# A decoder layer with routed experts: first expert for the last token tile without scatter and read, down bias stacked and added in memory, weight remainders and last rank in another order

## The chip, the cores and the metric

The kernel runs on one core of a Trainium2 chip. Its metric is the device time of one execution in microseconds (us). The engines are TensorE (PE, with its weight loads as PEld), VectorE (DVE), ScalarE (ACT), GpSimd (POOL) and SyncE (SP, which issues most DMAs). Each works through its own list in order and waits on semaphores.

## The reference

One layer of three parts, each added to its input and normalised: causal self-attention with 16 heads, a cross-attention with a linear feature map, and a mixture of 8 experts of which each token takes 2. There are 8 x 112 = 896 tokens of 512 numbers. The part that the change touches is the last:

```python
logits = h @ router_weight.T + router_bias
top_vals, top_idx = jax.lax.top_k(logits, TOP_K)
top_w = jax.nn.softmax(top_vals, axis=-1)
scores = jnp.zeros_like(logits).at[jnp.arange(T)[:, None], top_idx].set(top_w)
...
glu = gate * jax.nn.sigmoid(gate * ALPHA)
act = (up + 1.0) * glu
expert_out = jnp.einsum('eti,eih->eth', act, down_proj) + down_proj_bias[:, None, :]
out = jnp.einsum('te,eth->th', scores, expert_out)
```

## The kernel before, in words

The 896 tokens are 7 tiles of 128 (NT = 7); a row of 512 numbers is KC = 4 blocks of 128. Weights and operands of the large products are split into a high part (rounded to fp32r, by ACT: `split_hi`) and a remainder (by DVE: `split_lo`, line 1420); `products` (line 315) runs three matmuls per block, high x high, high x remainder, remainder x high. So weights of an expert are ready when ACT (`gu_high`, `dn_high`) and DVE (`gu_low`, `dn_low`) have been over them.

Routing goes tile by tile: `cross_out` and `cross_add` finish the second part, `x2_norm(n)` writes the tile's row, PE turns it (`turn_x2`, line 799), ACT copies it (`x2_copy`), PE computes the logits (`router`, line 806), DVE picks two experts (`choose`, lines 1623 to 1647), PE ranks the tokens (`rank`, lines 816 and 817), DVE computes slots and scores (`assign`, lines 1653 to 1668), and POOL scatters each row twice into `x_rows` in memory (`scatter`, line 508). Each expert has a region of ROWS slots there; the first CAP = 288 are read for it. After the scatter of all seven tiles SP reads experts 0 to 2 (`rows_in`, lines 431 and 433), then the scores and token numbers (`meta`, line 440). The order of these steps on PSUM banks is written out in `route_order`.

The down bias is handled ahead of the experts: scores are transposed (`turn_scores`, `scores_high`, `scores_low`), `down_bias(n)` multiplies them by the 8 x 512 bias in three matmuls over 8 partitions, DVE adds the row (`bias_add`, line 1673), and SP stores the sum as the start of `y_acc` in memory (`base_store`).

Then the experts. For expert e, PE transposes the rows read (`gather(e, k)`, line 973, three pieces of 128, 128 and 32 rows; ACT and DVE make high part and remainder), runs four parts of 24 matmuls (`gate_up_part(e, q)`), and the down products of the expert before (`down(e - 1, k)`, 36 matmuls). For each part DVE clamps (`clamp`, lines 1900 and 1904), ACT takes the sigmoid, POOL multiplies (`gated`, line 529), DVE multiplies again (`hidden`, line 1913), and ACT and DVE split the result (`h_high`, `h_low`). ACT scales the down results (`y_evac`, line 1329) and POOL adds them to `y_acc` with an indirect DMA (`add_rows`, line 546). Banks 0 to 3 hold the parts, 4 to 7 gathers and down results. Expert 7 is combined by one-hot matmuls with rows of `y_acc` read back, and the last normalisation and the stores follow.

On ACT and DVE the order inside an expert is written out by hand; `SPLITS` says behind which part the next expert's gate and up weights are split. On DVE it ends with the last `gu_low`s and `dn_low(e)`, on ACT with the `gu_high`s, `y_evac(e-1, 0)`, `y_evac(e-1, 1)`, `dn_high(e)`, `y_evac(e-1, 2)`.

## Time and profile before

| what | value |
|---|---|
| median of three timed runs | 865.51 us (865.08 to 868.34) |
| the profiled execution | 868.03 us, span 866.2 us |
| busy PE, PEld | 836.4 us (97%), 734.4 us (85%) |
| busy DVE, ACT, POOL | 479.2 us (55%), 319.2 us (37%), 97.2 us (11%) |
| mean granted TensorE clock | 0.98 |
| DMA | 97.39 MB, mean 112 GB/s |

The span runs from the first to the last instruction of the profiled execution; a little lies around it. A busy PE is not PE at its peak: matmuls are pipelined, and a matmul at half the clock counts as busy for twice as long. The page draws the span in 40 slices with the granted clock of each. The chain that ended last gives 11% of the span to PE at line 315 and 1% each to DVE's split of weights at line 1420 and to the reads of the down weights. Waits are given as idle time ahead of an instruction with the one that ended it.

### The profile page before, as it was taken

How to read it: one execution, taken by the hardware profiler on the slowest of the kernel's cores; microseconds unless marked ns; L12 is line 12 of the kernel's file. 1: busy time of each engine (PE TensorE's matmuls, PEld its weight loads, DVE VectorE, ACT ScalarE, POOL GpSimd, SP SyncE). 2: the span in 40 equal slices, each digit the busy share in tenths (PEclk: the TensorE clock that was granted, in tenths of full speed). 3: DMA queues.
4: the chain of work that ended last, by engine and by line, in shares of the span. 5: the costliest groups of instructions: out<-in, count | busy, mean ns of one | idle time of the engine just before them, and what ended most of it. 6: DMA issues, size and time to landing. Idle time of an engine off the chain costs nothing. (4 is left out here: it accounts for less than half of the span.)

```text
span 866.2 us, 12601 instructions
## 1 busy us (share of the span) xinstructions
PE 836.4 (97%) x4913; PEld 734.4 (85%) x4913; DVE 479.2 (55%) x877; ACT 319.2 (37%) x718; POOL 97.2 (11%) x92
## 2 busy tenths in 40 slices
PE   7999999999999999999999999999988999999995
PEld 6989898989899898978799878888866888888883
DVE  4435445363635464484860343455677677777765
ACT  4443324242333333342352222122233365555434
POOL 0000000000000000000000000110221244343331
PEclk9999999999999999999999999999975999999998
DMA  9990644614030003003110011110187366665225
GB/s 322 345 298 6 200 136 140 192 55 148 6 98 6 25 8 122 1 6 133 50 36 0 2 36 36 61 48 14 61 330 223 125 201 195 178 198 160 65 49 184
DMA packets 35758, 97.39 MB, mean 112 GB/s; under 512 B 6664, under 2 KB 9224, under 8 KB 33008
## 3 DMA queue, kind: packets, MB, share of 16 engines
q1 hardware_dynamic: 32224, 88.69, 30.5%
q0 software_dynamic: 3472, 7.87, 4.5%
q8 instruction: 40, 0.66, 0.3%
q14 instruction: 22, 0.18, 0.1%
HBM read 64.10 MB, written 31.53 MB: 110 GB/s over the span
## 5 line engine op out<-in xcount | busy, mean ns | idle before, releaser
L315 PE MATMUL bank<-w_kv,cT 128*125 128x512 f32 x576 | 143.5, 400 | 0.0
L315 PE MATMUL bank<-xT,w_qkv 128*128 128x512 f32 (+1 forms) x672 | 137.8, 365 | 0.2 <-ACT qT L1117 0.2
L315 PEld LDWEIGHTS bank<-xT,w_qkv 128*128 128x128 f32 x672 | 122.1, 188 | 15.2 <-ACT qT L1117 0.5
L315 PEld LDWEIGHTS bank<-w_kv,cT 128*125 128x125 f32 x576 | 104.1, 186 | 23.7
L315 PE MATMUL bank<-x_g,w_gu 128*128 128x288 f32 x768 | 109.7, 301 | 3.6 <-DVE x_g L1420 2.9
L315 PEld LDWEIGHTS bank<-x_g,w_gu 128*128 128x128 f32 x768 | 105.5, 192 | 5.5 <-issue 3.2
L499 POOL TENSOR_TENSOR ln_rs<-ln_ve,half 128x1 f32<-128x1 f32 (+2 forms) x16 | 11.2, 704 | 628.6 <-DVE ln_ve L1549 614.9
L315 PE MATMUL bank<-w_o,zT 128*128 128x512 f32 x336 | 79.8, 395 | 0.5 <-DVE acc L1755 0.5
L315 PE MATMUL bank<-w_qkv,xT 128*128 128x256 f32 x588 | 77.3, 287 | 0.0
L315 PEld LDWEIGHTS bank<-w_o,zT 128*128 128x128 f32 x336 | 61.7, 188 | 15.1 <-DVE acc L1454 1.8
L315 PEld LDWEIGHTS bank<-w_qkv,xT 128*128 128x128 f32 x588 | 72.2, 191 | 0.0
L315 PE MATMUL bank<-w_dn,hT 128*128 128x512 f32 (+1 forms) x288 | 68.5, 396 | 0.0
L315 PEld LDWEIGHTS bank<-w_dn,hT 128*128 128x128 f32 (+1 forms) x288 | 46.0, 161 | 19.3
L1420 DVE TENSOR_TENSOR w_qkv<-raw_w,w_qkv 128x1024 fp32r<-128x1024 f32 x21 | 25.7, 1225 | 60.5 <-ACT w_qkv L1085 60.5
L1127 ACT ACTIVATE prob<-prob,neg_max 112x112 f32<-112x112 f32 x128 | 47.8, 375 | 21.9 <-DVE neg_max L1471 21.9
L1154 ACT ACTIVATE relu_c<-bank 125x512 f32<-125x512 f32 x24 | 14.4, 598 | 111.0 <-PE bank L315 111.0
L1137 ACT CAST zT<-bank 128x448 fp32r<-128x448 f32 x32 | 17.0, 533 | 92.5 <-PE bank L695 92.5
L1420 DVE TENSOR_TENSOR w_gu<-raw_gu,w_gu 128x1024 fp32r<-128x1024 f32 x32 | 48.4, 1523 | 0.5 <-ACT w_gu L1085 0.5
L1454 DVE TENSOR_TENSOR acc<-acc,bank 128x512 f32<-128x512 f32 x49 | 33.6, 685 | 24.3 <-PE bank L315 24.3
L1515 DVE SCALAR_TENSOR_TENSOR phi_k<-exp_c,relu_c 125x512 f32<-125x512 f32 x24 | 16.6, 691 | 48.1 <-ACT exp_c L1155 48.1
L529 POOL TENSOR_TENSOR pr<-gl,sg 128x288 f32<-128x288 f32 x32 | 32.8, 1025 | 87.7 <-ACT sg L1318 87.5
L1443 DVE COPY V<-bank 128x512 f32<-128x512 f32 (+1 forms) x32 | 20.0, 625 | 39.9 <-PE bank L315 39.9
(171 smaller groups left out, 1206.8 us busy)
## 6 DMA issues: line engine op xcount, KB each, us to landing
x_rows<-blank SPq DMA_DIRECT2D x9, 2084.0 KB, 15.6
raw_gu<-in_w_gu_dram SPq DMA_DIRECT2D x8, 2048.0 KB, 7.8
raw_w<-in_w_qkv_dram SPq DMA_DIRECT2D x22, 512.0 KB, 8.3
raw_dn<-in_w_down_dram SPq DMA_DIRECT2D x8, 1024.0 KB, 9.4
raw_c<-in_ctx_t_dram SPq DMA_DIRECT2D x8, 750.0 KB, 4.4
raw_o<-in_w_o_dram SPq DMA_DIRECT2D x8, 512.0 KB, 4.1
xg<-x_rows SPq DMA_DIRECT2D x8, 512.0 KB, 5.7
raw_kv<-in_w_kv_dram SPq DMA_DIRECT2D x2, 1024.0 KB, 6.8
```

The costliest lines, as they stand in the source:

```text
L315: last = nc.tensor.matmul(mm_out, lhs(a, k), rhs(b, k), start=(k == 0 and i == 0), stop=(k == n - 1 and i == 2))
L499: nc.gpsimd.tensor_tensor(ln_rs[:, ln, n0:n1], ln_ve[:, ln, n0:n1], half[:, n0:n1], ALU.pow)\
L529: nc.gpsimd.tensor_tensor(pr[:, q % 2], gl[:, q % 2], sg[:, q % 2], ALU.mult)\
L1127: e = nc.scalar.activation(prob[0:S, g, j, :], prob[0:S, g, j, :], ACT.Exp, bias=neg_max[0:S, i:i + 1], scale=-1.0, accum_out=exp_sum[0:S, ...
L1137: nc.scalar.copy(zT[:, 0, h, hf * HALF:(hf + 1) * HALF], banks[6 + g % 2][:, 0:HALF])\
L1154: nc.scalar.activation(relu_c[0:CM, n % 2, :], bank("ck", n)[0:CM, :], ACT.Relu)
L1420: return nc.vector.tensor_tensor(dst, src, bits(hi), ALU.subtract)
L1443: nc.vector.tensor_copy(V[:, p % 2, 2 * j:2 * j + n, :], banks[(1 + j) % 2][:, 0:n * 2 * E].rearrange("p (a c) -> p a c", a=n))\
L1454: nc.vector.tensor_tensor(acc[:, n, :], acc[:, n, :], banks[n % 2][:, :], ALU.add)\
L1515: nc.vector.scalar_tensor_tensor(phi_k[0:CM, n % 3, :], exp_c[0:CM, n % 2, :], 1.0, relu_c[0:CM, n % 2, :], ALU.min, ALU.add).then_inc(m[" ...
```

## The change

Expert 0 of the last tile (END = 6) leaves the common way. Its 128 tokens go through expert 0 as a dense tile straight from the turned row `x2T`: `x_end` (high part by ACT, remainder by DVE), 24 products of 128x512 and two bias matmuls from a one-row bias `bias_end` into banks 1 and 3 (`end_gate_up`), clamp, sigmoid and products (`end_clamp`, `end_swish`, `end_hidden`), a turn into bank 6 (`end_turn`), split (`end_h_high`, `end_h_low`), 12 down products into bank 0 (`end_down`) and a scaled add into the tile's bias row (`end_add`). For these tokens the slot of expert 0 is one past all regions (`offs_end`), and they are not counted there. Expert 0's rows can thus be read after six tiles' scatters (`row_out`); experts 1 and 2 wait for the seventh (`end_out`).

The down bias becomes one matmul over 72 partitions: the scores stand three times (`score3`), the bias as high part, remainder and high part. ACT copies the result (`bias_copy`), the base stored to `y_acc` is the row alone, and POOL adds the bias to it by an indirect add (`add_bias`). `add_rows` waits for seven adds more (ADDED).

The order changes: `choose(5)` stands before `x2_norm(6)`, `rank(6)` inside the dense products, the split of weights of expert 0 and 1 elsewhere, expert 1's gathers one part later, a sigmoid early on ACT. Cut to its core:

```diff
-            last = [("rk", 4), ("st", 0), ("t1", 5), ("rt", 5), ("t1", 6), ("rk", 5), ("rt", 6), ("db", 0), ("rk", 6),
-                    ("cnt", 0), ("db", 1), ("db", 2), ("st", 1), ("db", 3), ("db", 4), ("db", 5), ("db", 6)]
+            last = [("rk", 4), ("st", 0), ("t1", 5), ("rt", 5), ("db", 0), ("rk", 5), ("t1", 6), ("rt", 6), ("rk", 6),
+                    ("db", 1), ("st", 1), ("db", 2), ("db", 3), ("db", 4), ("db", 5), ("db", 6), ("cnt", 0)]
-        SPLITS = {0: ((3,), (), (), (), ()), 1: ((), (), (), (0,), (1, 2, 3))}
+        SPLITS = {0: ((1,), (2,), (3,), (), ()), 1: ((), (), (), (0,), (1, 2, 3))}
@@ SP
             def base_store(n):
-                sp.wait_ge(*done("db", n))
-                sp.dma_start(y_acc[n * P:(n + 1) * P, :], acc[:, n, :]).then_inc(base_out, 16)
+                sp.wait_ge(m["row_ok"], n + 1)
+                sp.dma_start(y_acc[n * P:(n + 1) * P, :], row[:, n, 0:D]).then_inc(base_out, 16)
...
+                sp.dma_start(bias_end[0:1, :].rearrange("o (c p) -> o c p", p=P),
+                             t["gu_b"].rearrange("p e c -> e c p")[0:1]).then_inc(in_bias, 16)
...
-            sp.wait_ge(*ready("wo", NT - 1))
-            sp.dma_start(raw_gu[1], t["w_gu"][1]).then_inc(in_gu[1], 16)
...
-            sp.wait_ge(row_out, 16 * 2 * NT)
-            for e in range(3):
+            for n in range(4, NT):
+                base_store(n)
+            sp.wait_ge(row_out, 16 * 2 * END)
+            rows_in(xg[0], 0, in_xg[0])
+            sp.wait_ge(*ready("wo", NT - 1))
+            sp.dma_start(raw_gu[1], t["w_gu"][1]).then_inc(in_gu[1], 16)
+            sp.wait_ge(end_out, 16 * 2)
+            for e in range(1, 3):
@@ POOL
+            def add_bias(n):
+                if n < END:
+                    pool.wait_ge(*done("db", n))
+                else:
+                    pool.wait_ge(m["end_dve"], 7)
+                nc.gpsimd.indirect_dma_start(y_acc, bass.IndirectOffsetOnAxis(ap=ids[:, n:n + 1], axis=0),
+                                             acc[:, n, :], None, bounds_check=T + DUMP - 1, oob_is_err=True,
+                                             compute_op=ALU.add).then_inc(add_done, 16)
+            pool.wait_ge(base_out, 16 * (NT + 1))
+            for n in range(4):
+                add_bias(n)
             for e in range(NE + 1):
                 if e < NE:
                     for q in range(KC):
                         gated(e, q)
+                        if e == 0 and 4 + q < END:
+                            add_bias(4 + q)
                 if e == 1:
-                    pool.wait_ge(base_out, 16 * (NT + 1))
+                    add_bias(END)
                     pool.wait_ge(in_meta, 64)
                 if e and e < NE:
                     add_rows(e - 1, lambda k, rows: meta[0:rows, k, e - 1, NE:NE + 1], lambda k: (3 * (e - 1) + k) % 4)
@@ PE, down bias and the dense tile
-                products(o[:, :], lambda a, k: scoreT[a][0:NE, n * P:(n + 1) * P], lambda b, k: dn_b[b][0:NE, :], 1)\
+                nc.tensor.matmul(o[:, :], scoreT[0:STACK, n * P:(n + 1) * P], dn_b[0:STACK, :], start=True, stop=True)\
...
+            end_gate_up(0, 0, 0, 2)
             rank(6)
+            end_gate_up(0, 0, 2, KC)
             down_bias(1)
+            pe.wait_ge(m["end_dve"], 1)
+            pe.wait_ge(in_bias, 16)
+            end_gate_up(1, 0)
+            for h in range(2):
+                nc.tensor.matmul(banks[END_BANK[h]][:, :], all_ones[0:1, :], bias_end[0:1, h * D:(h + 1) * D],
+                                 start=False, stop=False)
+            turn_scores(1)
             down_bias(2)
+            down_bias(3)
@@ PE, experts
+            gather(0, 0)
+            gather(0, 1)
+            pe.wait_ge(m["gu_lo"], KC)
+            end_gate_up(0, 1).then_inc(m["end_mm"], 1)
+            down_bias(4)
+            down_bias(5)
+            gather(0, 2)
+            down_bias(6)
+            count()
             for e in range(NE):
                 pe.wait_ge(m["gu_lo"], KC * e + KC)
                 pe.wait_ge(m["xg_lo"], 3 * e + 3)
                 for q in range(KC):
+                    if e == 0 and q == 1:
+                        pe.wait_ge(m["end_dve"], 3)
+                    if e == 2 and q == 0:
+                        pe.wait_ge(m["end_dve"], 7)
                     gate_up_part(e, w_gu[e % 2], x_g[e % 2], q)
-                    if e == 0 and q + 1 < KC:
-                        gather(1, q)
-                    if q and e and e + 1 < NE:
+                    if e == 0 and q == 0:
+                        end_turn()
+                    if q and e + 1 < NE:
                         gather(e + 1, q - 1)
+                if e == 1:
+                    end_down()
                 if e:
                     for k in range(3):
                         down(e - 1, k)
@@ ACT, before and at the start of the experts
             x2_copy(5)
+            gu_high(0, 0, 2)
+            gu_high(0, 0, 3)
+            top_tanh(5)
             x2_copy(6)
...
+            split_hi(x_end[:, 0], x2T[:, END % 2]).then_inc(m["end_act"], 1)
+            bias_copy(0)
...
+            bias_copy(4)
+            bias_copy(5)
+            gather_high(0, 2)
+            end_swish()
+            bias_copy(6)
+            gu_high(1, 1, 0)
+            end_h_high()
@@ DVE
             cross_stats(6)
+            choose(5)
             x2_norm(6)
-            choose(5)
             assign(5)
+            gu_low(0, 0, 0)
+            split_lo(x_end[:, 1], x2T[:, END % 2], x_end[:, 0]).then_inc(m["end_dve"], 1)
             choose(6)
+            gu_low(0, 0, 1)
             assign(6)
...
+            gather_low(0, 0)
+            gather_low(0, 1)
+            gather_low(0, 2)
+            end_clamp()
+            levels()
+            end_hidden()
+            gu_low(1, 1, 0)
...
                 if more:
                     dn_low(e, e % 2)
+                if e == 1:
+                    end_add()
```

## Rows read from the trace of the kernel before

**Rows 1.** The page: the span, and PE's line of part 1.
```profile
span 866.2 us, 12601 instructions
...
PE 836.4 (97%) x4913; PEld 734.4 (85%) x4913; DVE 479.2 (55%) x877; ACT 319.2 (37%) x718; POOL 97.2 (11%) x92
```

**Rows 2.** The chain in order of time: start, us, what (count).
```profile
719.23 14.93 PE bank L315 x84
...
741.97 14.93 PE bank L315 x84
```

**Rows 3.** Timeline of the last tiles: start, us, engine, line, operation [idle before <-releaser].
```profile
639.97 0.55 DVE L1554 TENSOR_SCALAR row<-acc,ln_mv,ln_rs 128x512 f32<-128x512 f32 x1 [0.69 <-POOL ln_rs L499]
...
643.44 0.17 DVE L1668 CAST slot_u<-slot_f 128x2 uint32<-128x2 f32 x1
...
644.50 0.17 DVE L1623 TENSOR_TENSOR logit<-bank,rt_b 128x8 f32<-128x8 f32 x1 [0.90 <-PE bank L806]
...
647.66 0.17 DVE L1668 CAST slot_u<-slot_f 128x2 uint32<-128x2 f32 x1
...
648.63 0.97 POOL L508 DMA_INDIRECT x_rows<-row,slot_u  x1 [1.88 <-DVE slot_u L1668]
...
653.72 0.38 SPq L431 DMA_DIRECT2D xg<-x_rows  x1
...
658.97 2.50 PE L973 MATMUL bank<-ident,xg 128*128 128x128 f32 x12 [2.55 <-DMA xg<-x_rows]
```

**Rows 4.** Busy time by stretch: stretch, us, PE, PEld, DVE, ACT, POOL, clock, DMA.
```profile
640.00:641.00 1.00, 0.42 (x2) 0.43 (x3) 0.93 (x6) 0.00 (x0) 0.00 (x0) 0.54 1.03 442
667.00:668.00 1.00, 1.00 (x8) 1.00 (x7) 0.05 (x1) 0.00 (x0) 0.00 (x0) 0.81 1.04 371
855.00:857.00 2.00, 1.16 (x6) 0.62 (x4) 1.93 (x8) 1.73 (x4) 1.04 (x2) 1.00 0.28 101
858.00:859.00 1.00, 0.00 (x0) 0.00 (x0) 0.96 (x7) 1.00 (x3) 0.54 (x1) 0.76 0.17 62
```

**Rows 5.** Timeline of PE in expert 0.
```profile
662.60 5.56 PE L315 MATMUL bank<-x_g,w_gu 128*128 128x288 f32 x24 [1.13 <-DVE x_g L1420]
...
668.36 3.44 PE L315 MATMUL bank<-x_g,w_gu 128*128 128x288 f32 x24
...
680.94 6.64 PE L315 MATMUL bank<-x_g,w_gu 128*128 128x288 f32 x48 [1.77 <-DVE x_g L1420]
```

**Rows 6.** Indirect DMAs by stretch (725, 704 to 705, 646): count, us to landing.
```profile
y_acc<-y,meta POOLq DMA_INDIRECT x1, 4.9
...
y_acc<-y,meta POOLq DMA_INDIRECT x1, 7.8
...
x_rows<-row,slot_u POOLq DMA_INDIRECT x1, 2.9
```

**Rows 7.** Groups by line and shape: PE at line 729, count, busy us, mean ns.
```profile
L729 PE MATMUL bank<-v_c,phi_k 125*128 125x132 f32 x192 | 25.7, 278 | 0.0
```

**Rows 8.** Timeline from expert 1 to expert 2.
```profile
695.61 8.61 PE L315 MATMUL bank<-w_dn,hT 128*128 128x512 f32 x36
...
704.12 1.89 ACT L1085 CAST w_dn<-raw_dn 128x2048 fp32r<-128x2048 f32 x1
...
704.75 6.67 PE L315 MATMUL bank<-x_g,w_gu 128*128 128x288 f32 x48 [0.53 <-DVE w_gu L1420]
...
706.04 2.29 DVE L1420 TENSOR_TENSOR w_dn<-raw_dn,w_dn 128x2048 fp32r<-128x2048 f32 x1 [1.35 <-ACT w_dn L1085]
```

**Rows 9.** Timeline of POOL, DVE and PE in experts 2 and 3.
```profile
711.12 2.42 POOL L529 TENSOR_TENSOR pr<-gl,sg 128x288 f32<-128x288 f32 x2
...
712.41 0.46 DVE L1913 SCALAR_TENSOR_TENSOR hh<-up,pr 128x288 f32<-128x288 f32 x1
...
718.80 0.43 PE L973 MATMUL bank<-ident,xg 32*128 32x32 f32 x4
...
727.18 1.54 POOL L546 DMA_INDIRECT y_acc<-y,meta  x1 [0.30 <-issue]
```

More of the change, by code:

```diff
@@ L240, in decoder_layer @@
         row_out = sem("row_out")
+        end_out = sem("end_out")
         add_done = sem("add_done")
@@ L1192, in top_tanh, with bias_copy @@
                     .then_inc(m["tw_ok"], 1)
+            def bias_copy(n):
+                act.wait_ge(*ready("db", n))
+                act.wait_ge(m["row_ok"], n + 1)
+                nc.scalar.copy(acc[:, n, :], bank("db", n)[:, :]).then_inc(done("db", n)[0], 1)
             def scores_high(i):
@@ L1359, in _ @@
                         dn_high(e, e % 2)
-                if e and more:
+                if more:
                     gather_high(e + 1, 2)
@@ L1873, in _, with levels @@
-            bias_add(1)
-            gu_low(0, 0, 0)
-            scores_low(1)
-            bias_add(2)
-            gu_low(0, 0, 1)
-            bias_add(3)
-            gu_low(0, 0, 2)
-            bias_add(4)
-            gu_low(0, 0, 3)
+            gu_low(0, 0, 2)
+            gu_low(0, 0, 3)
+            scores_low(1)
+            def levels():
+                dve.wait_ge(*ready("cnt", 0))
+                nc.vector.tensor_reduce(most[:, 0:1], bank("cnt", 0)[:, 0:NE], AX.X, ALU.max)\
+                    .then_inc(done("cnt", 0)[0], 1)
+                dve.wait_ge(*done("cnt", 0))
+                for j in range(ROUNDS - 1):
+                    nc.vector.tensor_scalar(most[:, j + 1:j + 2], most[:, 0:1], float((j + 1) * CAP), None, ALU.is_gt)\
+                        .then_inc(m["put_ok"], 1)
+                dve.wait_ge(m["put_ok"], 3 * NT + ROUNDS - 1)
+                nc.vector.tensor_reduce(most[:, 4:5], most[:, 1:4], AX.X, ALU.add).then_inc(m["put_ok"], 1)
+                dve.wait_ge(m["put_ok"], 3 * NT + ROUNDS)
+                nc.vector.tensor_copy(more_i[:, :], most[:, 4:5]).then_inc(m["more_ok"], 1)
@@ new lines, in end_h_low, with end_add @@
+            def end_h_low():
+                dve.wait_ge(m["end_act"], 3)
+                split_lo(h_end[:, 1], banks[6][:, :].rearrange("p (k c) -> p k c", k=KC), h_end[:, 0])\
+                    .then_inc(m["end_dve"], 1)
+            def end_add():
+                dve.wait_ge(m["end_mm"], 3)
+                dve.wait_ge(*done("db", END))
+                nc.vector.scalar_tensor_tensor(acc[:, END, :], banks[0][:, :], row[:, END, D:D + 1], acc[:, END, :],
+                                               ALU.mult, ALU.add).then_inc(m["end_dve"], 1)
@@ L1942, in _ @@
                 hidden(e, KC - 1)
-                if e and more:
+                if more:
                     gather_low(e + 1, 2)
```

204 lines of the change are left out of this document (123 added, 81 removed).

## The prediction, made before the changed kernel was built

> **What bounds the kernel now.** I read the page first, then the chain that ended last, then the stretch 636 to 720 us engine by engine. The span is 866.2 us [rows 1]; the profiled execution took 868.03 us, the three timed ones 865.08 to 868.34, median 865.51. Below I work out a difference in us and add it to span and median alike.
>
> TensorE (PE) is busy 97% of the span [rows 1], and from expert 2 on the chain of waits repeats with PE products from one expert to the next, 719.23 and 741.97, so 22.74 us an expert [rows 2]. No gap of PE there is large enough to repay a delay, so whatever time PE loses or wins before expert 3 should reach the end unchanged. That leaves one place where the change works: from the last token tile's router to expert 3.
>
> There the reader is to see three things. First, PE waits for the scatter: the last tile's slots are ready at 647.83, its first scatter starts at 648.63, the read of expert 0's rows is issued at 653.72, and PE gets them at 658.97 [rows 3]. Second, the granted clock falls to 1.2 GHz at 640.5, after a stretch of little matrix work, and is back at 2.4 GHz only at 667.2 [rows 4], 4.6 us after the dense products began at 662.60 [rows 5]. Third, expert 0 to expert 1 costs PE another 1.77 us of waiting for the remainder of expert 1's rows [rows 5].
>
> **Start of expert 0 (S0).** The change reads expert 0's rows after six tiles. The sixth tile's slots are ready at about 643.6 [rows 3], so with two issues and a landing of 2.9 us [rows 6] the read goes out near 649, and with the 5.2 us between read and first transpose [rows 3] the rows are there at 654. The wait for DMA is gone. What is late next is PE and ACT work, which I walk through. VectorE (DVE) now does choose(5) (ten small instructions of 0.1 to 0.2 us, an estimate of 1.2) before x2_norm(6), so the last row is ready at 641.7, not 640.5. From row to logits it was 4.0 us [rows 3], with one rank more in front 4.2: the logits come at 645.9. PE then puts 8 of the new 128x512 products around rank(6). 24 matmuls of 288 columns take 5.56 us nearly all at the low clock, 3.44 at the high one [rows 5]; 36 of 512 columns take 8.61 at the high one [rows 8]. So 512 columns cost 0.24 us high and 0.41 low. Eight products, rank and one bias matmul are 3.3 + 1.0 + 0.4 = 4.7 us, to 650.6. With the 4.6 us seen before, the clock comes back just then. The rest at 0.24: 8 products 1.9; two bias matmuls in plain f32, which come as two instructions each, 192 of 132 columns taking 25.7 us [rows 7], hence 0.14 each and about 0.45 at 512 columns, 1.8 together; transposed scores 0.4, two bias products 0.5, two gathers 0.7, 8 products 1.9, two bias products 0.4: 658.2. ACT then copies two bias tiles (0.6 each) before the third gather's copy, and DVE takes its remainder: 660.0, S0 = 660.2, 2.4 us early. If the short matmuls of rank(6) delay the clock by one more step it is 661.2. I take 2.0 early. Bounds: with the high clock throughout, DVE and ACT alone put S0 at 657.4 (5.2 early); with the low clock throughout it is 665 (2.5 late).
>
> **What the removal of bias work is worth.** 21 matmuls become 7; at the low clock 14 x 0.41 = 5.7 us of PE. But they stood in front of rows that only arrived at 658.97, so before, they cost nothing, and now they make room for the 26 added products. The seven adds of DVE become seven copies on ACT (0.6 each, in the walk above) and seven indirect adds on POOL. Splits of weights that move from before 657 into expert 0 (gu_high and gu_low of expert 1) lie beside 3.3 us parts and hide there. The row-wise bias of the last tile is read in 4-byte pieces and is one DMA with many packets; it has from 626 to 652 and delays only weights needed after 680. The three down-bias loads, memsets, wider score copies and earlier base stores (rows, not sums) are free by the same cover. If none of that holds, it is at most 1 us at S0.
>
> **Expert 0 to expert 1 (S1).** From 668.36 to 679.17 PE ran three parts and two of the gathers between them [rows 5], 3.6 us a part with gather, so four parts and three gathers take 14.2 us. New is the turn of the last tile's hidden rows behind part 0: DVE has clamp, levels and hidden products of about 3.6 us to do first, so PE waits 0.4 and turns for 0.4. Expert 1's gathers all move one part later, the last behind part 3, and there no down product covers them: two clamps, two hidden products, two remainders of rows and one of hidden rows at 0.3 to 0.7 each on DVE leave PE idle an estimated 3.4 us. 14.2 + 0.8 + 3.4 = 18.4 us. Before, S0 to S1 was 662.60 to 680.94, 18.34 [rows 5]. What the clock gives is eaten by the uncovered gathers: S1 stays 2.0 early, at 678.9.
>
> **Expert 1 to expert 2 (S2): +5.0.** Before, from S1: down products at +14.67, 36 of them in 8.61 us, expert 2 at +23.81 after 0.53 of waiting [rows 8]. Now 12 products of the last tile go first, a third of 8.61, 2.87 us. Expert 2 also waits for end_add, because the last tile's sum lies in bank 0. end_add stands on DVE behind dn_low(1), which waits for dn_high(1) on ACT, which stands behind y_evac(0,1), which waits for the second down piece. From S1: 14.67 + 3 x 2.87 = 23.28; copy 0.7; dn_high 1.89; dn_low 2.29 [rows 8]; end_add 0.7 (as other 128x512 adds): 28.85. That is 5.04 us more than 23.81. Nothing pays it back, as expert 2 has no idle PE time.
>
> **POOL in expert 2: +4.7.** add_bias(6) waits for end_add too, and add_rows(0) behind it waits for the landing of all seven bias adds. Behind these on POOL's queue stand three adds and then gated(2,0), for which DVE's hidden(2,0) waits. From S2: end_add -0.1, start 0.8 later (slots 647.83 to scatter 648.63 [rows 3]), landing L, wake 0.3, three adds at 1.54 + 0.30 [rows 9], gate an estimated 0.9: 7.4 + L. Before, hidden(2,0) ran at 712.41, 7.66 after S2 at 704.75, just after the first of the two gates that began at 711.12 [rows 9]. From there DVE had no slack: hidden, remainder of weights, clamp, remainder of rows, and PE's gather(3,2) starts at 718.80 in the instant the last of them ends [rows 9]. So PE stalls L - 0.2. Indirect adds landed 4.9 us after issue with quiet queues, 7.8 beside a weight load, scatters 2.9 [rows 6]. I take 4.9, as the nearest in kind: +4.7, bounds +2.7 and +7.6.
>
> The Trainium skill, DMA: Bandwidth & Descriptors, section "Anatomy of one DMA", gives about 2.0 us plus size over 436 GB/s for one such DMA, an estimate of 2.6 us for these 256 KB. The trace's 4.9 speaks against it; by the page the term would be +2.4 and the whole 873.2 (rival 1 takes it in).
>
> **The clock again: +2.3.** After PE's last matmul at about 856.2 the clock fell at 858.8 [rows 4]. The 4.7 us stall is longer than that stretch; if the clock falls in it, the low level would last as after 662.60, 4.6 us at half speed, 2.3 us. The waits of 3.4 and 2.7 us may or may not fall so; I count none. Bounds of this term 0 and 4.6.
>
> **Sum.** -2.0 + 5.0 + 4.7 + 2.3 = +10.0 us: span 876.2, median 875.5.
>
> **Rivals.**
> 1. The landing is hidden or short. For it: scatters landed in 2.9. Against: the adds took 4.9 and more [rows 6]. POOL's term and the fall of the clock go away or shrink: -2.0 + 5.0 = +3.0, 868.5; with half of it, 871.
> 2. It is faster. One mechanism: the added dense products hold or regain the high clock before 648. Then S0 is 5.2 early, expert 0's first part is already fast and its tail hides; the start is worth up to 5.2 + 2.1 + 1.77 = 9.1 us (first part 5.56 against 3.44, and the idle of 1.77 [rows 5]), against +5.0: -4.1, 861.4; with ACT and DVE also done 2.4 us earlier at S2, since their splits there start earlier, 859, which I take for it. It decides only if the clock is up before 648 and POOL's landing is covered. Against: it falls at 640.5, before any new product.
> 3. More of the same: the clock also falls in the waits before S1 and S2, or the add lands beside the 1 MB weight load in 7.8 us. 10.0 + 2.3 + 2.9 = +15.2, 880.7.
> 4. The change does not do what it says: the early read queues behind base stores, or the clock stays low through 660, and S0 is not early at all but up to 2.5 late. 10.0 + 2 to 4.5: 877.5 to 880.
>
> **How the numbers follow.** Forecast 0.52; rival 1 0.22; rival 2 0.06; rival 3 0.12; rival 4 0.08. The range holds the forecast, rival 1, rival 4 and the near half of rival 3: 867.5 to 881. A measurement of this kernel tells some 0.5% (4.3 us) from no change: 861.2 to 869.8 is "same". Faster gets rival 2 and a rest, 0.06; same gets the part of rival 1 without any stall and some of the forecast's low edge, 0.2; slower 0.74.
>
> **What would show it.** In the profile after: PE's first part of expert 0 near 660.6 at the high clock; the granted clock back at 650 to 654; 18.4 us from there to expert 1; 28.9 us from expert 1 to expert 2 with PE's wait put down to DVE's add into the last tile's row; POOL idle before three adds in expert 2 on a DMA's landing; PE idle 4 to 5 us before the small gather of expert 3; then 22.8 us per expert. The prediction is wrong if end_add ends before the down pieces do, if POOL's gates of expert 2 run before DVE wants them, or if the clock never falls to begin with.

## The result, and the profile after

| | before | after |
|---|---|---|
| median of the runs | 865.36 us (865.08 to 868.34, 4 runs) | 880.72 us (880.49 to 881.28, 4 runs) |
| ratio to before | | 1.017, 95% interval 1.0157 to 1.0183 |
| the profiled execution, its span | 868.03 us, 866.2 | 881.28 us, 879.5 |

The change costs 15.4 us where 10 were forecast. The page of the kernel after, the lines that answer to [rows 1]:

```profile
span 879.5 us, 12708 instructions
...
PE 843.1 (96%) x4943; PEld 740.0 (84%) x4943; DVE 482.1 (55%) x889; ACT 324.9 (37%) x729; POOL 106.3 (12%) x99
```

TensorE (PE) has only 6.7 us more of busy time than in [rows 1], on a span 13.3 us longer. About half of the loss is new idle time, and some of the rest is products that ran at half the clock. To find the places, I read the start of the same step in both traces. S0 to S3 are the starts of experts 0 to 3 on PE.

| point on PE | before | after | later by | this step alone | forecast for the step |
|---|---|---|---|---|---|
| S0 | 662.60 | 662.51 | -0.1 | -0.1 | -2.0 |
| S1 | 680.94 | 681.97 | +1.0 | +1.1 | 0 |
| S2 | 704.75 | 712.94 | +8.2 | +7.2 | +5.0 |
| small gather of expert 3 | 718.80 | 731.60 | +12.8 | +4.6 | +4.7 |
| S3 | 727.60 | 741.90 | +14.3 | +1.5 | +2.3 |

From S3 on the delay goes through to the end, but for 1 us that the tail of the profiled execution gives back. The medians are 15.4 us apart and not 13.3, because the profiled execution of before lay 2.7 us above its median and that of after 0.6.

**The start.** Timeline of PE in the kernel after, the last tile up to S0 (start, us, engine, line, operation [idle before <-releaser]), against [rows 3, 5]:

```profile
643.20 1.88 PE L843 MATMUL bank<-rt_w,x2T 128*128 128x8 f32 x8 [0.67 <-ACT x2T L1271]
...
649.77 3.62 PE L1004 MATMUL bank<-w_gu,x_end 128*128 128x512 f32 x8
653.31 1.98 PE L1021 MATMUL bank<-bias_end,all_ones 1*128 1x512 f32 x4
...
656.06 1.32 PE L1044 MATMUL bank<-ident,xg 128*128 128x128 f32 x8
657.03 3.50 PE L1004 MATMUL bank<-w_gu,x_end 128*128 128x512 f32 x8
...
662.51 0.76 PE L326 MATMUL bank<-x_g,w_gu 128*128 128x288 f32 x4 [0.60 <-DVE x_g L1528]
```

The wait for DMA of [rows 3] (2.55 us before the first transposes) is gone, as intended: the transposes at 656.06 wait for nothing. But eight products of 512 columns took 3.50 us at 657.03. Busy time by stretch of the same kernel (the clock is the third figure from the end) tells why, beside [rows 4]:

```profile
642.00:643.00 1.00, 0.53 (x4) 0.29 (x4) 0.97 (x8) 0.44 (x1) 0.00 (x0) 1.00 1.02 394
643.00:644.00 1.00, 0.80 (x4) 0.80 (x4) 1.00 (x2) 0.97 (x3) 0.52 (x1) 0.51 1.00 382
652.00:653.00 1.00, 1.00 (x4) 0.56 (x2) 0.00 (x0) 0.00 (x0) 0.79 (x1) 0.50 0.99 363
653.00:654.00 1.00, 1.00 (x3) 0.44 (x3) 0.00 (x0) 0.00 (x0) 0.78 (x1) 0.87 1.00 369
656.00:657.00 1.00, 1.00 (x9) 0.94 (x8) 0.56 (x1) 1.00 (x3) 0.00 (x0) 0.84 1.14 325
659.00:660.00 1.00, 1.00 (x4) 0.81 (x3) 0.03 (x1) 0.00 (x0) 0.69 (x2) 0.50 0.98 254
660.00:661.00 1.00, 1.00 (x5) 0.52 (x5) 0.00 (x0) 0.20 (x1) 0.90 (x1) 0.96 1.13 213
...
680.00:681.00 1.00, 0.00 (x0) 0.00 (x0) 0.76 (x2) 0.37 (x2) 0.00 (x0) 0.78 0.88 377
...
731.00:732.00 1.00, 0.40 (x4) 0.40 (x4) 1.00 (x3) 0.10 (x1) 0.00 (x0) 0.88 0.95 410
```

The granted clock falls to 1.2 GHz at 643.0 and is back at 2.4 GHz at about 653.2. It is low once more from 656.7 to 660.0, and this time PE had been busy without a gap. The last two rows belong to later stages: the clock falls at about 680.6, in the wait before expert 1, and at about 731.8.

**The loads.** Issues of GpSimd (POOL) and SyncE's queue (SPq) in the kernel after:

```profile
648.01 0.38 SPq L450 DMA_DIRECT2D xg<-x_rows  x1
...
649.38 1.25 POOL L531 DMA_INDIRECT x_rows<-row,slot_u  x1 [3.31 <-DVE score L1782]
649.47 0.42 SPq L459 DMA_DIRECT2D raw_gu<-in_w_gu_dram  x1
650.93 0.97 POOL L531 DMA_INDIRECT x_rows<-row,slot_u  x1 [0.30 <-ACT acc L1282]
...
660.79 0.38 SPq L450 DMA_DIRECT2D xg<-x_rows  x1
```

The last tile is scattered by two indirect DMAs, at 649.38 and 650.93. The landing of the first (from issue, us), against the 2.9 of [rows 6]:

```profile
x_rows<-row,slot_u POOLq DMA_INDIRECT x1, 9.9
```

Expert 0's rows are read at 648.0, one us sooner than I forecast. But the 2 MB load of expert 1's weights now goes out at 649.47, in the same instant as the last tile's scatter. The scatter lands 9.9 us after issue, its second half 9.8, at 660.7, and expert 1's rows, whose read waits for both, are asked for at 660.79. I had not looked at this at all.

**Expert 0 to expert 2.** Timeline of PE, ScalarE (ACT) and VectorE (DVE), kernel after, against [rows 5, 8]:

```profile
677.73 0.43 PE L1044 MATMUL bank<-ident,xg 32*128 32x32 f32 x4 [0.85 <-DVE x_g L1528]
681.97 9.05 PE L326 MATMUL bank<-x_g,w_gu 128*128 128x288 f32 x48 [3.81 <-issue]
...
698.57 3.04 PE L326 MATMUL bank<-w_dn,h_end 128*128 128x512 f32 x12
701.45 8.50 PE L326 MATMUL bank<-w_dn,hT 128*128 128x512 f32 x36
...
707.80 1.89 ACT L1170 CAST w_dn<-raw_dn 128x2048 fp32r<-128x2048 f32 x1
709.73 2.29 DVE L1528 TENSOR_TENSOR w_dn<-raw_dn,w_dn 128x2048 fp32r<-128x2048 f32 x1 [2.06 <-ACT w_dn L1170]
711.94 0.74 DVE L2019 SCALAR_TENSOR_TENSOR acc<-bank,row,acc 128x512 f32<-128x512 f32 x1
712.94 6.62 PE L326 MATMUL bank<-x_g,w_gu 128*128 128x288 f32 x48 [3.00 <-DVE acc L2019]
```

The reader is to see two things: the last four rows are the chain high part of the down weights (ACT), remainder (DVE), `end_add` (DVE), expert 2 (PE), link by link; and two parts of expert 1 took 9.05 us where those of expert 2 took 6.62, because the clock fell in the 3.81 us of waiting.

**POOL in expert 2.** The rows that answer to [rows 9]:

```profile
713.46 1.56 POOL L578 DMA_INDIRECT y_acc<-acc,ids  x1 [13.16 <-DVE acc L2019]
...
719.47 1.58 POOL L568 DMA_INDIRECT y_acc<-y,meta  x1 [4.45 <-issue]
...
724.12 2.04 POOL L552 TENSOR_TENSOR pr<-gl,sg 128x288 f32<-128x288 f32 x2
725.43 1.05 DVE L2052 SCALAR_TENSOR_TENSOR hh<-up,pr 128x288 f32<-128x288 f32 x1 [4.89 <-POOL pr L552]
...
731.60 0.54 PE L1044 MATMUL bank<-ident,xg 32*128 32x32 f32 x4 [4.77 <-DVE x_g L1528]
```

The add of the last tile's sum is issued at 713.46, the three adds of rows behind it wait until 719.47, the gate product behind them runs at 724.12, DVE has waited 4.89 us for it and PE 4.77.

### The profile page after: what moved, and what is told of

Read it like the earlier page. It is cut to its first block and busy times, and to the rows that moved or that the text cites. A ratio compares the mean times of both kernels' runs of the same rounds, so it can differ in the third digit from the quotient of the medians.

```text
span 879.5 us, 12708 instructions
## 1 busy us (share of the span) xinstructions
PE 843.1 (96%) x4943; PEld 740.0 (84%) x4943; DVE 482.1 (55%) x889; ACT 324.9 (37%) x729; POOL 106.3 (12%) x99
## 5 line engine op out<-in xcount | busy, mean ns | idle before, releaser
L522 POOL TENSOR_TENSOR ln_rs<-ln_ve,half 128x1 f32<-128x1 f32 (+2 forms) x16 | 11.2, 704 | 628.3 <-DVE ln_ve L1657 615.1
L1239 ACT ACTIVATE relu_c<-bank 125x512 f32<-125x512 f32 x24 | 14.3, 598 | 110.4 <-PE bank L326 110.4
```

The costliest lines, as they stand in the source:

```text
L522: nc.gpsimd.tensor_tensor(ln_rs[:, ln, n0:n1], ln_ve[:, ln, n0:n1], half[:, n0:n1], ALU.pow)\
L1239: nc.scalar.activation(relu_c[0:CM, n % 2, :], bank("ck", n)[0:CM, :], ACT.Relu)
```

## The experiments

All are edits of the changed kernel. Each group of runs had its own runs of the kernel before; their medians were 866.03 us (e1 to e4), 865.78 (e6 to e9), 865.78 (e10 to e12) and 864.47 (e13).

| run | median us (range, runs) | ratio to before, 95% interval |
|---|---|---|
| e1_add_early | 871.13 (867.69 to 873.56, 10) | 1.0055 (1.0035 to 1.0075) |
| e2_pool_order | 877.41 (873.44 to 879.49, 4) | 1.0118 (1.0083 to 1.0153) |
| e3_gathers | 883.04 (882.22 to 884.12, 4) | 1.0202 (1.0175 to 1.0229) |
| e4_no_bias_row | 881.36 (881.08 to 882.32, 4) | 1.0182 (1.0156 to 1.0208) |
| e6_gath_gu | 879.72 (878.59 to 880.80, 4) | 1.0154 (1.0139 to 1.0169) |
| e7_add_gath_gu | 870.25 (867.27 to 872.62, 9) | 1.0048 (1.0032 to 1.0065) |
| e8_gu_behind | 869.70 (869.04 to 872.63, 4) | 1.0040 (1.0026 to 1.0055) |
| e9_add_gu | 873.12 (872.51 to 874.68, 4) | 1.0088 (1.0072 to 1.0104) |
| e10_splits | 872.24 (869.64 to 872.71, 5) | 1.0070 (1.0046 to 1.0094) |
| e11_gu_behind_no_bias | 871.07 (869.69 to 871.74, 5) | 1.0052 (1.0031 to 1.0073) |
| e12_bias_first | 871.51 (870.57 to 872.34, 4) | 1.0064 (1.0039 to 1.0089) |
| e13_add_gath_gu_bias | 871.10 (868.41 to 872.20, 6) | 1.0064 (1.0047 to 1.0081) |

### Is it the place of end_add? (e1_add_early)

```diff
                 h_low(e, KC - 1, hT[e % 2])
+                if e == 1:
+                    end_add()
                 for k in splits_at(e, KC):
                     gu_low(e + 1, (e + 1) % 2, k)
                 if more:
                     dn_low(e, e % 2)
-                if e == 1:
-                    end_add()
```

> Only DVE's order in expert 1 changes: end_add stands ahead of the three gu_low and dn_low(1). Theory (two joins on end_add): expert 2 waits for end_add, and POOL's bias add with its landing wait hangs on it too. From the profile of the changed kernel, expert 1 to expert 2 takes 30.97 us; without the wait of 3.0 it should be about 28.5, POOL's bias add of the last tile is issued some 7 us earlier and has landed before the rows of expert 0 are scaled, so the stall of 4.8 us ahead of expert 3's small gather and the fall of the clock behind it (10.01 us for 36 down products against 8.61) go as well: 3.0 - 0.5 + 4.6 + 1.4 = about 8.5 us less, 872.2 us. Rival: the stall in expert 2 comes from the three indirect adds themselves, which stand ahead of the gate products whatever they wait for; then only 2.5 us go, 878.2. Second rival: DVE is the bound there, and end_add only pushes the weight remainders back: 880 to 881.

Measured 871.13, 9.6 us less than the changed kernel, where 8.5 were expected; neither rival took place. PE's timeline of this run:

```profile
681.95 8.63 PE L326 MATMUL bank<-x_g,w_gu 128*128 128x288 f32 x48 [3.81 <-issue]
...
709.34 6.55 PE L326 MATMUL bank<-x_g,w_gu 128*128 128x288 f32 x48
...
723.62 0.43 PE L1044 MATMUL bank<-ident,xg 32*128 32x32 f32 x4 [0.47 <-DVE x_g L1528]
```

The 3.00 us before expert 2 are gone and the 4.77 before the small gather are down to 0.47, with the fall of the clock that followed. One DVE instruction of 0.74 us in the wrong place of its queue was 9.6 of the 15.4 us. Expert 1 starts as before the edit, so the start is a question of its own.

### Is it POOL's order? (e2_pool_order)

```diff
-                pool.wait_ge(add_done, ADDED + 48 * (c - 1 if later else c))
+                pool.wait_ge(add_done, 16 * END if isinstance(c, int) and c == 0 else ADDED + 48 * (c - 1 if later else c))
...
+                        if e == 2 and q == 2:
+                            pool.wait_ge(add_done, 16 * END + 48)
+                            add_bias(END)
                 if e == 1:
-                    add_bias(END)
```

> Only POOL's order changes: the last tile's bias add goes behind the third gate product of expert 2, and expert 0's row adds wait for six bias adds, not seven. Theory: the stall of 4.8 us ahead of expert 3's small gather is the landing of that one add (5.3 us from 713.46 to 718.7) in front of POOL's gate products; it goes, and with it the fall of the clock behind it (1.4 us). Expert 1 to expert 2 stays at 31 us. 880.7 - 4.6 - 1.4 = 874.7 us. Rival (the adds themselves hold POOL up): row adds start at once, but the gates still stand behind them; under 1 us goes, 880. If the landing wait only moves to the third gate, the gain is given back in expert 3: 878 to 880.

Measured 877.41: 3.3 us less than the changed kernel, not the 6 forecast. The stall at the small gather of expert 3 is gone (it ran at 727.87 without a wait), so that mechanism holds; the 3.00 us before expert 2 stand, and this time the clock fell in them:

```profile
712.34 8.14 PE L326 MATMUL bank<-x_g,w_gu 128*128 128x288 f32 x48 [3.00 <-DVE acc L2021]
```

That is 1.5 us more for two parts than the 6.62 of the changed kernel, behind the same wait of the same length, and 1.4 us came back as a wait in expert 3. Expert 0 started at 658.85, 3.7 us earlier, and met a wait of 2.30 for expert 1's rows. The trace is that of the slowest of four runs, which lie between 873.44 and 879.49, so the split of the missing 2.7 us holds for that one execution.

### Is it the late gathers? (e3_gathers)

```diff
+                    if e == 0 and q + 1 < KC:
+                        gather(1, q)
-                    if q and e + 1 < NE:
+                    if q and e and e + 1 < NE:
                         gather(e + 1, q - 1)
```

and the same on ACT and DVE: expert 1's gathers stand behind parts 0, 1 and 2 again.

> Only expert 1's gathers change: they stand behind parts 0, 1 and 2 of expert 0 on PE, ACT and DVE as in the kernel before, not behind parts 1, 2 and 3. Theory: the wait of 0.85 + 3.81 us between part 3 and expert 1 is the last gather's remainder with no down product to cover it; it shrinks to about the 1.8 us of the kernel before, and the clock, which fell at 680.8 in that wait, stays up, so expert 1's first two parts take 6.6 us, not 9.05. 2.8 + 2.4 = 5.2 us less: 875.5 us. Rival: the read of expert 1's rows, issued only at 660.8, lands too late for a gather at 666, PE waits there for DMA instead, and the gain is 0 to 2.5 us: 878 to 881. Then the idle time has only moved.

Measured 883.04, slower than the changed kernel. I had expected a gain; the mechanism of the rival took place, and it cost 2 us more than the rival's own figure. Expert 0 started at 658.26, and then:

```profile
668.17 1.09 PE L1044 MATMUL bank<-ident,xg 128*128 128x128 f32 x4 [6.00 <-DMA xg<-x_rows]
...
683.37 6.63 PE L326 MATMUL bank<-x_g,w_gu 128*128 128x288 f32 x48 [2.19 <-issue]
```

Expert 1's rows, read at 661.11, are not there at 662. So the late gathers of the change fit its late rows, and putting them back alone makes it worse. The last wait before expert 1 did shrink, from 3.81 to 2.19, and the clock did not fall in it. This pointed at the loads.

### Is it the bias row, or the clock? (e4_no_bias_row)

```diff
-            for h in range(2):
-                nc.tensor.matmul(banks[END_BANK[h]][:, :], all_ones[0:1, :], bias_end[0:1, h * D:(h + 1) * D],
-                                 start=False, stop=False)
```

This leaves out the gate and up bias of expert 0 for the last tile.

> Leaves out the two bias matmuls of the last tile's dense expert 0 (four PE instructions of one partition by 512 columns, f32), so those tokens lack that bias. Theory: they cost 1.9 us by themselves, and the second fall of the clock (0.84 at 656, back at 660) comes from them, because they use one row of the array; without them the last 8 products take 1.9 us, not 3.5. Expert 0 then starts near 659.5, not 662.5, 3 us less, if ACT's copies do not end last: 877.7 us. Rival 1: the clock falls for another reason (the copies and gathers around): only 1.9 us go, 878.8. Rival 2: ACT and DVE between third gather and part 0 set the start: 0 to 1 us.

Measured 881.36, no gain, although expert 0 started at 657.22, 5.3 us earlier, and the clock did not fall a second time:

```profile
667.02 0.66 PE L1041 MATMUL bank<-ident,xg 128*128 128x128 f32 x4 [2.69 <-DMA xg<-x_rows]
...
680.38 8.59 PE L326 MATMUL bank<-x_g,w_gu 128*128 128x288 f32 x48 [3.81 <-issue]
```

The four products alone don't make the clock fall a second time, since e2 and e3 kept them and had no second fall either; e8 and e11 below show that they have a part in it. What e4 does show is that 5.3 us at the start are worth 1.6 at expert 1, and nothing in the end: in this execution the 36 down products before expert 3 took 11.08 us where the kernel after took 10.01, because the clock was low for longer.

### Where may the 2 MB load stand? (e6, e9, e7, e8)

In e6, e7 and e9 the load of expert 1's weights goes out ahead of all the scatters of the last tile:

```diff
+            sp.wait_ge(*ready("wo", NT - 1))
+            sp.dma_start(raw_gu[1], t["w_gu"][1]).then_inc(in_gu[1], 16)
             for n in range(4, NT):
                 base_store(n)
             sp.wait_ge(row_out, 16 * 2 * END)
             rows_in(xg[0], 0, in_xg[0])
-            sp.wait_ge(*ready("wo", NT - 1))
-            sp.dma_start(raw_gu[1], t["w_gu"][1]).then_inc(in_gu[1], 16)
```

e6 has the gathers of e3 with it, e9 the early end_add of e1, and e7 both.

> The kernel with only expert 1's gathers moved back took 883.0 us: PE waited 6.0 us for expert 1's rows, whose read went out at 661.1. Here one thing more: the 2 MB load of expert 1's gate and up weights is issued ahead of the base stores and of the read of expert 0's rows, at about 637 as in the kernel before, not behind that read at 648.6. Theory: the load shares the DMA engines with the last tile's scatter, which then lands 9.9 us after issue where it took 2.9 to 3.8 before, and SP reads expert 1's rows only after it. With the load gone from there the scatter lands in 3 to 5 us, the read goes out near 655, PE's wait for DMA goes, and expert 1 starts near 677, not 683.4; the joins on end_add stay. 883.0 - 6 = 877 us. Rival: the scatter is slow of itself or queued behind POOL's other adds; the read stays near 661 and the time at 883.

> end_add early and the weight load first, with the changed kernel's own later gathers. Tells whether the gathers' place costs anything once the rows are there: theory, the uncovered last gather costs PE 3.8 us of waiting ahead of expert 1 and in some runs the clock behind it, so this stays near the 871.1 of end_add alone, 3 to 5 us above the version with the earlier gathers. Rival: the later gathers are harmless and the time is that of the other version within 1 us.

> end_add early, gathers as in the kernel before and the weight load first, together. If the three causes stand apart from one another: 883.0 - 6 for the load and - 9.6 for end_add (880.7 to 871.1 when alone), 867.4 us; with the clock up through expert 0 and 1, 2 us less, 865.5, about the kernel before. Rival: with PE no longer waiting there, DVE's splits of expert 1's weights bound expert 0 (four parts of 3.3 us hold three gathers, four weight remainders and the last tile's work), expert 1 does not start before 680, and the time stays at 870 to 871.

e6 measured 879.72, 3.3 us less than e3 and not the 6 forecast. Its gathers no longer wait for a DMA, so the load was what they had met, but expert 0 started 6.7 us later than in e3, at 664.94. e9 measured 873.12 and gained nothing on e1 (2 us slower by the medians), since the late gathers don't use the earlier rows. e7 measured 870.25: with the load moved, the early gathers are worth 2.9 us (e9 to e7), about what e9's text said (3 to 5). But e7 is at its rival's 870 to 871, not at the 867.4 forecast, and the start is part of the reason: the sixth tile's scatter, now beside the load, lands in 7.1 and 7.7 us (3.5 and less in e8), expert 0's rows are read at 651.35, PE waits for them until 656.10, and expert 0 starts at 663.18.

In e8 the load stands behind the read of expert 1's rows, the rest is as in e7:

```diff
-            sp.wait_ge(*ready("wo", NT - 1))
-            sp.dma_start(raw_gu[1], t["w_gu"][1]).then_inc(in_gu[1], 16)
...
             for e in range(1, 3):
                 rows_in(xg[e], e * ROWS, in_xg[e])
+                if e == 1:
+                    sp.wait_ge(*ready("wo", NT - 1))
+                    sp.dma_start(raw_gu[1], t["w_gu"][1]).then_inc(in_gu[1], 16)
```

> As the kernel before in this list, but the load of expert 1's gate and up weights is issued behind the read of expert 1's rows (near 656), so the last tile's scatter also has the queues to itself. Theory: scatter lands in 3 to 5 us; but the weights land near 664 to 667 and ACT, which wants the first quarter near 661, waits for them with the last tile's hidden rows behind it: 1 to 3 us later than with the load first, 868 to 870 us. Rival (place of the load does not matter so long as it is not beside the scatter): the same time within 0.5 us.

Measured 869.70. The figure lies inside what was expected, but not for the reason given: e8 was to be 1 to 3 us later than e7, and it is 0.55 earlier, which is the rival (the place does not matter so long as it is not beside the scatter), with intervals that overlap. Issues of SyncE's queue, and the landing of the last tile's scatters, in e8:

```profile
648.24 0.38 SPq L450 DMA_DIRECT2D xg<-x_rows  x1
...
654.24 0.38 SPq L450 DMA_DIRECT2D xg<-x_rows  x1
...
655.26 0.45 SPq L463 DMA_DIRECT2D raw_gu<-in_w_gu_dram  x1
```

```profile
x_rows<-row,slot_u POOLq DMA_INDIRECT x2, 3.4
```

The scatter lands in 3.4 us instead of 9.9 and expert 1's rows are read 6.5 us sooner: the load was the cause of the slow landing. Its gain in time is small all the same, and the next runs ask why.

### What holds expert 1 back? (e10, e11, e12, e13)

e10 is e8 with another spread of the weights' remainders:

```diff
-        SPLITS = {0: ((1,), (2,), (3,), (), ()), 1: ((), (), (), (0,), (1, 2, 3))}
+        SPLITS = {0: ((1,), (2, 3), (), (), ()), 1: ((), (), (), (0,), (1, 2, 3))}
```

> e8_gu_behind with one thing more: of the three splits of expert 1's weights that lie in expert 0, two stand behind part 1 and none behind part 2 (before: one behind each of parts 0, 1, 2). In e8 TensorE ended the last part of expert 0 at 677.7, VectorE clamped it only at 679.7, because it was busy with a weight remainder of 1.2 us and hidden rows of 0.45, and TensorE waited 3.6 us for the remainder of the last rows. Theory (my step 'splits hide beside the parts' is what fails there): the clamp comes 1.7 us earlier, the wait falls to about 1.9, as the 1.77 of the kernel before, and the time from 869.7 to 868.0. Rival (VectorE is simply full in expert 0): the two splits together delay the clamps of part 2, TensorE waits for banks there, and nothing is gained: 869.5 to 870.

Measured 872.24, no gain on e8 (2.5 us slower by the medians, with intervals that overlap); the rival was right in kind. PE waited 4.08 us before expert 1 against 3.58 in e8, since the two remainders delay the clamps of part 2, then part 3 and everything behind it on DVE.

e11 is e8 with the cut of e4, so it too leaves out that bias.

> e8_gu_behind without the four bias products of the last tile's expert 0 (the gate and up bias of that expert is left out for that tile). It repeats e4_no_bias_row where expert 1's rows are read early (read issued at 654.2 in e8). In e4 expert 0 started 5.3 us earlier and all of it went into the wait for expert 1's rows. Theory (an early start does reach the end once the rows are there): expert 0 starts 2 us earlier, or 5 where the clock stays up, and the time is 867.7 to 864.7. Rival (another wait takes its place: the 2 MB load now issued at 655.3 lands near 663.5, and the engines that split it stand still before their first clamp): expert 0 starts earlier, expert 1 does not, 869 to 870.

e12 is e10 with the bias products ahead of the last tile's others, and no longer behind them:

```diff
             router(5)
             down_bias(0)
+            for h in range(2):
+                pe.wait_ge(free[END_BANK[h]], LAST[END_BANK[h]])
+            pe.wait_ge(in_bias, 16)
+            for h in range(2):
+                nc.tensor.matmul(banks[END_BANK[h]][:, :], all_ones[0:1, :], bias_end[0:1, h * D:(h + 1) * D],
+                                 start=True, stop=False)
             rank(5)
```

> e10_splits, and the bias products of the last tile's expert 0 stand ahead of its other products, before the rank of tile 5, where TensorE waits 1.0 us for the choice and 0.7 for the logits. Theory: 1.98 us of products leave the walk to expert 0, at most 1 us of them delays the router; expert 0 starts 1 to 2 us earlier, or 3 to 5 where the clock does not fall a second time: 866 to 867, or down to 864. Rival (the router's chain is what sets the scatter and the rows): everything moves 1 to 2 us later, 869 to 870.

Measured 871.07 and 871.51. Expert 0 started at 659.10 and 657.48, 3.7 and 4.4 us earlier than in e8 and e10, and expert 1 at 681.29 and 681.06, where it was: the rival of e11, right in both. The theory of e11 (867.7 to 864.7) failed. For e12 I had expected 866 to 867, and its own rival (a delayed router) is not what happened: its reads went out at the same times as in e8. The chain in order of time, ACT, DVE and PE in e12:

```profile
655.02 10.70 DMA raw_gu<-in_w_gu_dram
```

```profile
665.74 1.04 ACT L1173 CAST w_gu<-raw_gu 128x1024 fp32r<-128x1024 f32 x1 [6.67 <-DMA raw_gu<-in_w_gu_dram]
666.82 1.23 DVE L1533 TENSOR_TENSOR w_gu<-raw_gu,w_gu 128x1024 fp32r<-128x1024 f32 x1 [6.21 <-ACT w_gu L1173]
...
668.95 4.97 PE L326 MATMUL bank<-x_g,w_gu 128*128 128x288 f32 x24 [3.50 <-DVE up L2048]
```

The load lands 10.7 us after issue; both splitting engines stand still for it for over 6 us, and PE, which needs DVE's clamps to get a bank, waits 3.50.

e8 and e11 also say something on the second fall of the clock. They differ by the four bias products, and in both traces the clock is back at about 653.5. The last eight products of the tile then took, in e8 and in e11:

```profile
657.27 3.50 PE L1005 MATMUL bank<-w_gu,x_end 128*128 128x512 f32 x8
```

```profile
655.02 2.10 PE L1005 MATMUL bank<-w_gu,x_end 128*128 128x512 f32 x8
```

With the bias products the clock fell again at 656.9, without them it stayed at 1.00. The same holds in all traces: where these products stand in the walk and the clock came back at 650.5 or later (after, e1, e6, e7, e8, e10), it fell again; where it was back by 649 (e2, e3), or where the products are absent or placed earlier (e4, e11, e12), it did not fall again before expert 0. In e9 and e13 PE had waited for rows first. It is one trace of each, so this is a pattern and not a cause shown.

e13 takes the early load of e7 and the early bias products of e12.

> e7_add_gath_gu with the bias products of the last tile's expert 0 ahead of its other products, as in e12_bias_first. In e12 expert 0 started at 657.5 instead of 661.9, and expert 1 at 681.06 instead of 680.94, because the 2 MB of expert 1's weights, issued at 655, landed 10.7 us later. In e7 these weights are loaded ahead of the scatter and the early start would meet no late weights. Theory (expert 1's start hangs on its rows and weights, and both are early here): expert 0 starts 1.5 to 2.5 us earlier than the 663.2 of e7, expert 1 about as much earlier than 680.55, and the time is 868 to 869 against the 870.25 of e7. Rival (the scatter and the read of expert 0's rows, slowed by the load, set the start, 656.1 in e7): expert 0 starts at most 0.5 us earlier and the time is 870 to 871.

Measured 871.10, the rival's mechanism and its upper figure. PE's timeline:

```profile
657.10 1.94 PE L1044 MATMUL bank<-ident,xg 128*128 128x128 f32 x8 [4.52 <-DMA xg<-x_rows]
...
664.63 3.42 PE L326 MATMUL bank<-x_g,w_gu 128*128 128x288 f32 x24 [0.57 <-DVE x_g L1532]
```

PE is ready for expert 0's rows at 652.6 and gets them at 657.10; the clock falls in that wait, and expert 0 starts later than in any run but e6.

Put together, the starts of experts 0 and 1 and what PE waited for most on the way (us):

| kernel | S0 | S1 | the wait |
|---|---|---|---|
| before | 662.60 | 680.94 | rows of expert 0, 2.55 |
| after | 662.51 | 681.97 | before expert 1, 3.81 |
| e2 | 658.85 | 681.61 | rows of expert 1, 2.30, then 3.81 |
| e3 | 658.26 | 683.37 | rows of expert 1, 6.00 |
| e4 | 657.22 | 680.38 | rows of expert 1, 2.69, then 3.81 |
| e7 | 663.18 | 680.55 | rows of expert 0, 1.31, then 2.45 |
| e8 | 662.76 | 681.25 | before expert 1, 3.58 |
| e11 | 659.10 | 681.29 | weights of expert 1, 2.69, then 2.81 |
| e12 | 657.48 | 681.06 | weights of expert 1, 3.50, then 3.40 |
| e13 | 664.63 | 682.00 | rows of expert 0, 4.52, then 2.45 |

The four that are not in the table (e1, e6, e9, e10) have S1 at 681.95, 682.32, 682.52 and 680.94. S0 moves over 7.7 us (657.22 in e4 to 664.94 in e6) and S1 over 3.0. Two groups lie in this. Where expert 0 starts before 660, PE meets a wait for expert 1's rows or weights, and the gain is used up. Where it starts at 661.9 or later no such wait of PE is left, and S1 does follow S0, at a distance that the order of the work sets: 17.37 us in e6, e7 and e13 (early load, early gathers), 19.46 in the kernel after, e1 and e9 (late gathers, wherever the load stands), 18.5 and 19.0 in e8 and e10 (where DVE's first remainder comes 1.6 to 1.7 us later than it could, for the late load), 18.34 before. No run has an early S0 and also the rows and weights of expert 1 in time. No version here is faster than the kernel before. The best, e8, is 1.004 (1.0026 to 1.0055) times its time, some 3.5 us; 2.9 us of that are the 12 down products that the last tile now has for itself.

## Why the prediction was right, and where it was wrong

The direction was right and the time lies in the range, but at its very edge, 880.7 of 867.5 to 881. The two largest terms held, and the sum was short by 5.4 us for reasons that the steps show. That the figure of rival 3 is 880.7 too is luck: of its two parts the clock before expert 1 took place, with 1.9 us, but the landing of 7.8 did not (5.3), and the rest of the 5.4 came from the start and from S0 to S1.

- **Expert 1 to expert 2, forecast +5.0: right, with a clock that I had not counted.** From the first down product to expert 2 it is 712.94 - 698.57 = 14.37 us; before, 9.14 [rows 8]; +5.2 against +5.04. The further 1.9 us are the slow clock of the two parts at 681.97. e1 shows the cause by taking it away.
- **POOL in expert 2, +4.7: right, +4.6.** The landing took 5.3 us (713.46 to the end of the wait at about 718.7) against 4.9. e2 took the stall away by POOL's order alone, e1 by an earlier add. The page that I weighed (the Trainium skill, DMA: Bandwidth & Descriptors, section "Anatomy of one DMA") gives about 2.6 us for these 256 KB as an estimate; the measured 5.3 speaks for the trace.
- **The clock in that stall, +2.3: right in kind, +1.5.** It fell at about 731.8, just after PE had started again, and 36 down products took 10.01 us against 8.61 [rows 8], 1.4 of the 1.5. But I counted none for the waits before S1 and S2. The clock fell in the first (3.81 us) and not in the second (3.00 us), while in e2, e3 and e4 it did fall in that same second wait. This is the mechanism of my rival 3, and here it is worth 1.9 us.
- **Start of expert 0, -2.0: wrong, -0.1.** The walk was sound up to its clock. The logits came at 645.1 (forecast 645.9), the read at 648.0 (649), the bias products took 1.98 us (1.8). The step that failed is "with the 4.6 us seen before, the clock comes back just then": it came back at 653.2 and not at 650.6, and fell again, and eight products took 3.50 us instead of 1.9. In e2, with the same code up to there, the clock was back at about 649 and S0 was 658.85, somewhat earlier than the 660.2 of my walk. So this part can differ between executions of the same code, and in this one rival 4 held (the clock low until 660, no earlier start).
- **"S1 stays 2.0 early": wrong for a reason that I had not looked at.** I took it that an earlier S0 is an earlier S1. S0 is earlier than before by 3.5 to 5.4 us in e2, e3, e4, e11 and e12, and S1 is never earlier than before by more than 0.6 us. The diff moves the load of expert 1's weights to just before the last scatter, and I did not cost that move, though I costed every compute step that was moved. The scatter's 9.9 us against 2.9 were my bounds' 2.9 to 7.8 for another DMA, in a place where I never asked.
- **18.4 us from S0 to S1: mis-sized, 19.5.** The idle time there was 0.85 + 3.81 = 4.7 us against 3.4 + 0.4. "Splits hide beside parts of 3.3 us" fails: in e8 DVE clamped the last part 2.0 us after its end, busy with a remainder and hidden rows. e10 shows no gain from moving them forward. DVE is busy 17.95 of the 19.46 us from S0 to S1, 92%, although its average is 55%. The late gathers themselves cost 2.1 us of this distance (19.46 in e9, 17.37 in e7).
- **"Removal of bias work costs nothing at S0": not told apart.** The first four of the seven adds in memory were issued behind the last scatter, from 652.2 on, beside the 2 MB load, and landed in 9.5, 8.9, 7.0 and 7.2 us; nothing waits for them before expert 2. No run took them away alone.

What of the 15.4 us is shown: the order of end_add on DVE 9.6 (e1 undoes it); the 12 down products 2.9 (their rows, not an experiment); the other 2.9 lie in the waits and the slow clock before and after S1, of which e8, by the place of the load and the gathers, gives back 1.3 (ratio to before 1.0055 in e1, 1.0040 in e8, with intervals that overlap, so that this gain is not shown). That an earlier start brings nothing because of its DMAs rests on the waits in e2, e3, e4, e11 and e12, and that the early load delays the start on e7 and e13, each read from one execution.

What stays open is what decides whether the clock falls in a given wait or for the second time after 656. The ten runs of e1 fall into two groups, 867.7 to 869.0 at a mean clock of 0.99 and 870.4 to 873.6 at 0.984 to 0.987; the code is the same, and there is a trace of only one of the ten, from the second group.

## What to carry to other kernels

When a step is taken out of the common path, its last small instruction (here a 0.74 us add) should stand in its engine's queue where its input is ready, not where the program text ends; two waits and a fall of the clock hung on it. Before an earlier start is counted as a gain, list the transfers that the next stage needs with the times at which they land. If rows and weights arrive later than the earlier start needs them, the start only moves the wait from one of them to the next. And a load that is moved is a change of its own: look at what is issued in the same microsecond.

## What the runs showed that I had not expected

- An indirect scatter of the last tile lands 2.9 to 3.8 us after issue when no load is issued with it (before and e8), and 9.9 us when a 2 MB load goes out 0.1 us later (kernel after). The load itself landed in 10.7 and 11.2 us in e12 and e8.
- TensorE's granted clock can fall with the engine busy: 656.7 to 660.0 in the kernel after, among bias, score and transposing products. In e3, where it was back at about 648.3, it stayed at 1.00. A row of e3 and one of the kernel after, PE alone (stretch, us, busy, clock, DMA share, GB/s):

```profile
656.00:660.00 4.00, 3.40 (x24) 1.00 0.94 281
```

```profile
656.00:660.00 4.00, 4.00 (x16) 0.58 0.99 306
```

- The same wait of 3.00 us before expert 2 cost no clock in the kernel after (two parts in 6.62 us) and 1.5 us in e2, e3 and e4 (8.14 to 8.15).
- Two remainders of weights on DVE, 1.22 us elsewhere, took 2.81 and 1.88 us at 670.88 and 675.20 in the kernel after, where POOL was issuing indirect adds and multiplying. They took 2.80 and 1.88 in e9 too, whose load stands elsewhere, but 1.21 to 1.51 in e7 and e8, which have the same POOL instructions and the early gathers. So the 2 MB load is not the cause; what in the order of the two engines is, no run tells.
